# Writing out the six looped batches of the retention stage of a hybrid attention kernel

## The reference

```python
xf = x.reshape(B, L, E)                                   # B = 8, L = 1024, E = 256, after a group norm
q = (xf @ Wq.T).reshape(B, L, H, KD).transpose(0, 2, 1, 3)             # H = 8 heads of 32
k = (xf @ Wk.T * SCALING).reshape(B, L, H, KD).transpose(0, 2, 1, 3)
vr = (xf @ Wv.T).reshape(B, L, H, HD).transpose(0, 2, 1, 3)
qr, kr = theta_shift(q, sin_q, cos_q), theta_shift(k, sin_k, cos_k)
qk = jnp.einsum('bhqd,bhkd->bhqk', qr, kr) * mask[None]
den = jnp.clip(jnp.abs(qk).sum(-1, keepdims=True), 1.0, 50000.0)
out = jnp.einsum('bhqk,bhkd->bhqd', qk / den, vr).transpose(0, 2, 1, 3)
out = (out - mu) / jnp.sqrt(var + LN_EPS) * ln_g + ln_b   # over each head
x = x + gelu(out) @ Wo.T
```

## Time and profile before

| | us |
|---|---|
| median of 3 runs | 2621.92 (2620.39 to 2627.72) |
| the profiled execution's own time | 2624.51 |
| its span in the trace | 2622.4 |
| mean granted clock of TensorE, of full speed | 0.984 |
| retention stage, bodies 0 to 7, weighted values of the first step to those of body 7's first | 48.64 to 987.02 |

### The profile page before, as it was taken

One profiled execution on the slowest core, in us unless ns is written; L12 is line 12 of the kernel. 1 busy time (PEld: TensorE's weight loads), 2 busy tenths in 40 slices (PEclk: granted clock), 3 DMA queues, 4 the chain that ended last, 5 costly groups with the idle time before them and its releaser, 6 DMA issues. The chain is left out here.

```text
span 2622.4 us, 43895 instructions
## 1 busy us (share of the span) xinstructions
PE 2512.7 (96%) x15328; PEld 1786.7 (68%) x15328; DVE 1834.2 (70%) x2847; ACT 1449.9 (55%) x2044; POOL 517.6 (20%) x444
## 2 busy tenths in 40 slices
PE   5999999999999999979999969999999999999999
PEld 2444444444444444369999958888888888888888
DVE  4878777777777777657777757666666666666665
ACT  2666565566566566636566545555555555555554
POOL 2333333333333333201212110000000000000000
PEclk8999999999999999989999979999999999999999
DMA  6232222222232222123223143000000000000000
GB/s 233 51 85 60 77 62 79 65 72 75 56 85 59 83 59 70 49 71 111 82 77 115 49 146 106 18 24 24 18 23 24 24 24 24 24 24 24 24 17 16
DMA packets 116786, 157.95 MB, mean 60 GB/s; under 512 B 16272, under 2 KB 82328, under 8 KB 116384
## 3 DMA queue, kind: packets, MB, share of 16 engines
q1 hardware_dynamic: 116640, 156.01, 20.1%
HBM read 72.03 MB, written 33.59 MB: 40 GB/s over the span
## 5 line engine op out<-in xcount | busy, mean ns | idle before, releaser
L488 DVE TENSOR_TENSOR l_prod<-l_scores,l_window 128x1024 f32<-128x1024 f32 x512 | 615.6, 1218 | 220.7 <-PE l_scores L325 186.0
L679 ACT ACTIVATE l_absp<-l_prod 128x1024 f32<-128x1024 f32 x512 | 521.9, 1053 | 282.8 <-PE l_den L350 233.6
L1696 ACT ACTIVATE e_r<-e_h,e_bn,e_rs 128x512 f32<-128x512 f32 x512 | 399.4, 781 | 485.7 <-PE e_h L1547 484.5
L325 PE MATMUL l_scores<-l_qst,l_kst 96*128 96x512 f32 x1024 | 369.3, 457 | 27.9 <-DMA l_qst<-l_lo 12.0
L325 PEld LDWEIGHTS l_scores<-l_qst,l_kst 96*128 96x128 f32 x1024 | 167.4, 190 | 288.3 <-issue 147.9
L1547 PE MATMUL e_y<-e_whi,e_h2lo 128*128 128x256 f32 x1024 | 289.8, 283 | 0.0
L1546 PE MATMUL e_y<-e_wlo,e_h2hi 128*128 128x256 f32 x1024 | 289.7, 283 | 0.0
L1545 PE MATMUL e_y<-e_whi,e_h2hi 128*128 128x256 f32 x1024 | 289.2, 282 | 0.1
L350 PE MATMUL l_den<-l_absp,l_ones 128*32 128x512 f32 x2048 | 274.7, 609 | 0.0
L339 PE MATMUL l_num<-l_prod,l_v 128*32 128x512 f32 x2048 | 269.3, 598 | 0.0
L1791 DVE CAST e_h1hi<-e_r 128x512 fp32r<-128x512 f32 x256 | 111.2, 434 | 224.3 <-ACT e_r L1696 220.2
(11 more groups left out here) (191 smaller groups left out, 4472.2 us busy)
## 6 DMA issues: line engine op xcount, KB each, us to landing
l_kst<-l_hi SPq DMA_DIRECT2D x256, 64.0 KB, 2.0
l_qst<-l_hi SPq DMA_DIRECT2D x256, 64.0 KB, 2.0
l_raw<-in_xT SPq DMA_DIRECT2D x8, 1024.0 KB, 5.6
l_kst<-l_lo SPq DMA_DIRECT2D x128, 64.0 KB, 2.0
l_qst<-l_lo SPq DMA_DIRECT2D x128, 64.0 KB, 2.0
l_xo<-in_x SPq DMA_DIRECT2D x32, 256.0 KB, 2.8
x_scratch<-l_xo SPq DMA_DIRECT2D x32, 256.0 KB, 2.3
l_xr<-x_scratch SPq DMA_DIRECT2D x8, 1024.0 KB, 8.0
```

The lines of the kernel that those rows point to most:

```text
L325: mm = nc.tensor.matmul(sc[j][:, s, :], kst[g][0:96, h, 128 * kt:128 * kt + 128], qst[c][0:96, h, :], start=True, stop=True)
L488: nc.vector.tensor_tensor(prod[n % 4][:], sc[j][:], win[:, 4 * g + 2 * j:4 * g + 2 * j + 2, w0:w0 + QC], ALU.mult).then_inc(prod_ready, 1)
L679: nc.scalar.activation(absp[n % 4][:], prod[n % 4][:], ACT.Abs).then_inc(abs_ready, 1)
L1696: nc.scalar.activation(r[m][:], p[m][:], ACT.Relu, bias=bn_[layer][1][:, m, e:e + 1], scale=rs[layer][:, m, e:e + 1]).then_inc(done, 1)
```

## The change

Five lines change. Each engine's loop over batches 1 to 6 becomes a loop of the program that writes the kernel, so that the six bodies stand one behind the other in each stream, with `b` a number. Nothing else is touched: order, buffers and waits of a body are the same.

```diff
@@ -206,7 +206,7 @@
             body(0, True, False)
-            with sp.Fori(1, B - 1) as b:
+            for b in range(1, B - 1):
                 body(b, False, False)
             body(B - 1, False, True)
@@ -436,7 +436,7 @@
             body(0, True, False)
-            with pe.Fori(1, B - 1) as b:
+            for b in range(1, B - 1):
                 body(b, False, False)
             body(B - 1, False, True)
@@ -635,7 +635,7 @@
             body(0, True, False)
-            with dve.Fori(1, B - 1) as b:
+            for b in range(1, B - 1):
                 body(b, False, False)
             body(B - 1, False, True)
@@ -745,7 +745,7 @@
             body(0, True, False)
-            with act.Fori(1, B - 1) as b:
+            for b in range(1, B - 1):
                 body(b, False, False)
             body(B - 1, False, True)
@@ -836,7 +836,7 @@
             body(0, True, False)
-            with pool.Fori(1, B - 1) as b:
+            for b in range(1, B - 1):
                 body(b, False, False)
             body(B - 1, False, True)
```

## The result

The changed kernel is slower: 2634.32 us median of 10 runs (2632.11 to 2640.19) against 2624.47 us of 10 runs before (2619.53 to 2627.84), a ratio of 1.0044 (of the means), 95% interval 1.0033 to 1.0055. The profiled execution took 2632.1 us, its span 2630.3. The forecast was 2606.5 us with a range of 2600 to 2614. So the kernel lost 10 us where it was to win 15 to 18.

A forecast was written before the change was run, and what follows sets the result against it. The prediction took PE, busy 96% of the span, as the bound. From the profiled time, 2624.5 - 13.6 (branches) - 3.3 (clock falls) = 2607.6 us, or 2605.0 from the median; forecast 2606.5 us, range 2600 to 2614.

The forecast's parts named there:

- PE's branches, 13.6 us less: Retention loop's body ends: without five taken branches, five closing steps fall from 37.12 to 23.50 us, 13.6 us less.
- The clock falls, 3.3 us less: Group-norm steps of the retention bodies: one fall to the lower clock instead of three, 1.63 us each, 3.3 us less.
- Register instructions, nothing, at most 1.4 us: Waits in the retention loop: removing their register instructions gains nothing, at most 1.4 us through DVE in the group-norm steps.
- The longer stream, nothing: PE's six retention bodies, instructions now coming once each: no cost taken; upper bound one stop of 2.4 us per body.
- The later stages of the same length: Sign that the forecast is right: stages after retention keep their length in the changed profile.
- the seven packets in body 6: Instruction queue in retention body 6: about seven packets a body, read as all engines together, 42 in six bodies.
- The sum: Whole kernel: 2624.5 - 13.6 - 3.3 = 2607.6 us, 2605.0 from the median; 2606.5 taken between.
- The rivals: Alternatives: no change 3%, standstill gone but more clock falls 8%, a late stack 4%, slower by instruction supply 3%.
- The slow one: Written-out retention bodies: instruction stream can't keep up, PE stops 2.4 us at each of 42 packets, about 2709 us; 3%.

The follow-up runs named there:

- the kernel with 70 and 64: Kernel before, loops untouched, with 70 increments of an unused semaphore at the start of PE's stream and 64 at its attention stage: 2610.39 us, ratio 0.9954.
- the kernels with 4 to 64: Changed kernel with 4, 8, 16 or 64 increments of an unused semaphore at the start of PE's stream: 2601.77, 2600.40, 2599.21 (again 2601.12), 2602.41 us.
- with 70: Kernel before, loops untouched, with 70 increments of an unused semaphore at the start of PE's stream only: 2618.90 us, ratio 0.9987.
- with 212: Changed kernel with 212 increments of an unused semaphore, 106 at the start of PE's stream and 106 at its attention stage: 2630.78 us.
- with 80: Kernel before, loops untouched, with 80 increments of an unused semaphore at the start of PE's attention stage: 2641.52 us, ratio 1.0071.

## Why the prediction was wrong

*PE's branches, 13.6 us less.* Right. All body ends are 4.70 us. But the reason given, that the branch costs it, was too short: the kernel with 70 and 64 takes the same branches in 0.2 us. What costs is the refetch, and the prediction did not ask why other taken branches of PE are short (L1656, 215 ns).

*The clock falls, 3.3 us less.* Right in kind, 4.9 us in size: none of seven passes fell in the profiled run. The number of falls is partly luck: the kernel with 70 and 64, whose bodies also lost their stall, has two.

*Register instructions, nothing, at most 1.4 us.* The bound was too low. The group-norm steps went from 7.63 to 7.39, and a body with the other engines looped takes, without stall or fall, 132.10 us against 131.7: 0.4 a body, 2.5 us in six. It was read from two steps, while two later steps of a body carry the rest.

*The longer stream, nothing.* **This is the step that failed.** "I take nothing, for written-out code is just what bodies 0 and 7 are." It asked what the longer stream does to the stage that is written out, and there nothing is just what it does: 131.68 us a body, with the packets landing underneath. It did not ask what it does to code behind it. "The later stages of the same length" stood under what would be right, and they were what failed: 33.6 us more in five bodies of the expert loop, 6.7 each, of which 4.4 is standstill and 2.4 TensorE at 1.2 GHz. The reading beside it was wrong too: the seven packets in body 6 are not those of all engines together but of PE's queue alone, so they could have told how many blocks a body of PE takes.

*The sum.* For the retention stage it was 13.6 + 3.3 = 16.9 us against 20.6 measured. With the expert loop kept the whole change gives 20 to 23 us (the kernels with 4 to 64), and with it refetched 20.6 + 5.1 - 33.6 = -7.9 us, the difference of the two spans.

*The rivals.* The slow one was on the right queue and in the wrong stage, and its price (a stop at each packet) was of another mechanism; it had 3%. None asked whether another loop loses what it holds.

*The signs that were there.* Two loops of PE are of nearly the same size, 1761 and 1592 records, and one had branches of 3854 ns and the other of 215. That a loop of 1592 ran without a packet of the instruction queue and one of 1761 didn't was in the trace of before, and the difference had to be explained before either was moved.

## What to carry to other kernels

On PE, a loop's cost at its branch was set in all these runs by whether its body was still held, so compare the branches of all loops of an engine before changing one: two loops near the size of what is held, one fast and one slow, mean that a shift of some instructions decides. Whoever writes code out, or adds any instruction to PE's stream, moves every later loop of it in its block (for the other engines no run here shows a price: DVE's branches took 67 ns at most); look at the later loops' branches and at the instruction queue's packets after each such edit. Here four useless instructions ahead of everything turned a loss of 0.4% into a gain of 0.8%, and 134 of them gave 0.5% with all loops left as they were, though only until the next edit of PE's stream moves them again.

## What was not expected of the hardware

A refetched loop costs 2.1, 2.5, 3.1 or about 7 us each time round (with 70, with 212, with 80, and in the changed kernel), at branches of nearly the same length (3.4 to 3.5 us at the median). By the places above, what differs is how many instructions of the loop stand in its first block. In the dearest case it is one to four: the idle time comes in one piece of 4.34 us and the granted clock of 1791 to 1805 us, around it, is 0.76. With 80 it is 16 to 19: the loop's first eight matmuls, each with its weight load, run between two pieces of 1.43 and 0.87 us, under which the clock stays at 1.00. The trace has two packets of the queue at each such branch, the second 3.1 to 3.2 us behind the first: they start at 1789.7 and 1792.8 in the changed kernel and at 1814.3 and 1817.5 with 80. The matmul behind the 4.34 us and the one behind the 0.87 us both start 2.4 to 2.5 us after the second packet's start. So a loop that has next to nothing in its first block waits for two packets in a row, which is how I read the price.

The clock doesn't always stay up behind the shorter pieces: with 212 the bodies have 135.1 us, and the two of five behind whose branch it fell have 137.1 and 137.2.

And the queue's packets alone, with no wait beside them, cost nothing that these runs show: the retention bodies written out take 131.7 us with them.
